# Edge pass of a graph layer with a feed-forward block: three chunks' statistics finished apart, and the second group's reciprocal root moved ahead of a gather

## The chip, the cores and the metric

One core of one Trainium2 chip runs the whole kernel in one launch. The metric is device time in microseconds (us). Before the change the median of three runs is 2741.15 us (2739.52 to 2741.22).

## What is computed

```python
def _layernorm(x, axis=-1, eps=1e-05):
    m = jnp.mean(x, axis=axis, keepdims=True)
    v = jnp.var(x, axis=axis, keepdims=True)
    return (x - m) / jnp.sqrt(v + eps)

# x: (50000, 768); src, dst: 25000 edges, sorted by dst; 12 heads of 64
def gnn(h, src, dst, W, attn_l, attn_r, W_res):
    hv = h.reshape(n, 12, 64)
    ft = jnp.einsum('nhd,od->nho', hv, W)
    a1 = jnp.sum(ft * attn_l, axis=-1)
    a2 = jnp.sum(ft * attn_r, axis=-1)
    e = jax.nn.leaky_relu(a1[src] + a2[dst], negative_slope=0.2)
    m = segment_max(e, dst)
    w = jnp.exp(e - m[dst])
    alpha = w / jnp.maximum(segment_sum(w, dst)[dst], 1e-16)
    agg = segment_sum(alpha[:, :, None] * ft[src], dst)
    return relu((agg + jnp.einsum('nhd,od->nho', hv, W_res)).reshape(n, 768))

x = x + gnn(_layernorm(x), src, dst, ...)
x = x + ffn(_layernorm(x))    # 768 -> 96 -> 768 with gelu; six class rows apart
```

## The kernel before

The kernel has two passes. The **edge pass** takes the 25,000 edges in 196 chunks of 128 (EC = 196), in groups of seven (G = 7) and turns of fourteen (BODY = 14). The **node pass** after it takes 392 tiles of 128 nodes. This change touches the edge pass alone, and there its first two turns.

Every engine has one program, written out by hand, that runs in order; the engines meet at semaphores. Each program loops over the same index `c` (turn `b`, place `i`) and does at `c` the work of chunk `c - LAG` for each of its steps. For one chunk the steps are:

- POOL (GpSimd) issues two gathers by index from `x` in HBM into rings of fourteen slots in `arena`: the 128 source rows (`xs_ring`, line 558, at place c) and the 128 target rows (`xd_ring`, line 536 in `gather_targets`, at place c + 3, DST_LAG). From chunk 14 on it also scatters row numbers into `row_scratch` (line 577), so that a place then has three issues.
- DVE (VectorE) takes mean and variance of the source rows (`source_stats`, lines 982 and 985) when the gather has landed. Once per group, at the place after the group's last chunk, it writes variance + eps of all seven chunks to `ve_s` (line 1061, semaphore `s_ve`).
- POOL raises the seven to the power -0.5 in one instruction into `r_s` (line 586 for the first group, line 592 for the others, at place 18 for the second group; semaphore `s_rp`).
- DVE makes the bias -mean * r in `nm_s` (line 1073, semaphore `s_nm`) and ACT (ScalarE) normalizes the chunk in place (line 668).
- PE (TensorE) transposes source and target rows (line 813), ACT copies the transposes out of PSUM (line 682), PE multiplies (lines 822, 850, 870), ACT copies out again (lines 688, 692) and squares the target rows for their variance (line 700).
- Once per group the attention follows. DVE writes the target variances to `ve_d` (line 1088), POOL raises them to the power -0.5 into `r_d` (line 549, at place 23 for the first group), DVE makes the scores `e_col` from that (lines 1185 to 1193, semaphore `s_leak`), and PE transposes them (line 837, at its place 19) and goes on.
- The sums over edges (lines 864 and 866) start at place 23.

Lines 1185 to 1193 stand in DVE's place 18 behind the statistics of chunk 18, so DVE does nothing else until `r_d` is there. In the same way line 837 stands in PE's program ahead of line 850 of chunk 9, the small product 870 and the transposes of chunk 11.

Ahead of the loop SP starts the loads of the constants and fourteen writes that fill `row_scratch` (3.2 MB, line 453). DVE makes small constants from PE's first products (lines 1020 to 1034). The weights `w1` and `w2` are loaded into the slots of `arena` that `ft_ring` (line 688's output) takes later, and split into high and low parts by DVE right after line 1061 of the first group.

Of the kernel before, what the change touches and what calls it, by code (L numbers as in the profile page):

```python
# [8 lines left out]
D = 768  # L9
# [48 lines left out]
DST_LAG = 3  # L58
HM = HEADS + 1
# [37 lines left out]
def exists(t, n):  # L97

    return not isinstance(t, int) or 0 <= t < n
# [8 lines left out]
def gnn_ffn_kernel(nc, x, x_cols, edges, dst_rows, dst_next, dst_prev, dst_ends, chunk_base, sel_heads,  # L108
# [9 lines left out]
    with ExitStack() as ctx:  # L118
# [60 lines left out]
        w2_sb = part(21504, D, rows=HID + 1)  # L179
        w1_sb = part(24000, NC, HID)  # L180
# [86 lines left out]
        with ExitStack() as edge:  # L267
            agg_ring = edge.enter_context(nc.sbuf_tensor("agg_ring", [P, AR, D], f32))
            dst_all = edge.enter_context(nc.sbuf_tensor("dst_all", [P, G * P], i32))
        row_init = agg_ring[:, AR - 1, 0:NT // BODY * RW].bitcast(i32)  # L270
# [261 lines left out]
        def _(pool):  # L532
# [6 lines left out]
            for b in turns(pool, NB, 2):  # L539
                for i in range(BODY):  # L540
# [21 lines left out]
                    if first and G <= c < G + 4:  # L562
                        for v in (2 * (c - G), 2 * (c - G) + 1):
                            gather_targets(v, v // G, e_all[:, v, 1:2])
                    if exists(cd, EC) and not (isinstance(cd, int) and cd < 8):
                        v = (i - DST_LAG) % BODY
                        e, kd = v // G, v % G
                        n = 2 * b + (i - DST_LAG) // G
                        at_least(pool, s_sqd, cd - BODY + 1)
                        settle(pool)  # L570
                        gather_targets(v, n, e_all[:, v, 1:2] if isinstance(cd, int) and cd < BODY else e_slot[:, e, kd, 1:2])
                        at_least(pool, s_sum, c - BODY - L_SUM + L_TR + 1)
                        settle(pool)
# [10 lines left out]
                    if isinstance(b, int) and c == G + 1:  # L584
                        pool.wait_ge(s_ve, 1)
                        pool.tensor_tensor(r_s[:, 0, :], ve_s[:, 0, :], half[:, 0:G], ALU.pow).then_inc(s_rp, 1)
                    gp = 2 * b + (i - 11) // G
                    if k == 11 % G and exists(gp, NG) and not (isinstance(gp, int) and gp == 0):
                        w = (i - 11) // G % 2
                        pool.wait_ge(s_ve, gp + 1)  # L590
# [63 lines left out]
        def _(act):  # L654
# [5 lines left out]
            for b in turns(act, NB, 2):  # L660
                for i in range(BODY):
                    c = BODY * b + i
                    cn = c - L_NORM
                    if exists(cn, EC):
                        v = (i - L_NORM) % BODY
                        w, k = v // G, v % G
                        act.wait_ge(s_nm, 2 * b + (i - L_NORM) // G + 1)
# [300 lines left out]
        def _(dve):  # L968
# [44 lines left out]

            dve.wait_ge(l_const, 16 * NCONST)
# [7 lines left out]
            for c in range(2):  # L1022
                source_stats(c, c, 0, c, 0)
# [10 lines left out]
            V.tensor_scalar(csr_neg[:], ps[:, 2, 0:P], -1.0, None, ALU.mult).then_inc(s_wgv, 1)  # L1034

# [7 lines left out]
            for b in turns(dve, NB, 2):  # L1043
                for i in range(BODY):
# [13 lines left out]
                    if k == 0 and exists(gv, NG):  # L1058
                        w = (i - 7) // G % 2
                        dve.wait_ge(s_ag, G * (gv + 1))  # L1060
                        V.tensor_scalar(ve_s[:, w, :], mvs[:, w, :, 1], EPS, None, ALU.add).then_inc(s_ve, 1)
# [7 lines left out]
                    if k == 1 and exists(gn, NG):  # L1069
                        w = (i - 8) // G % 2  # L1070
                        dve.wait_ge(s_rp, gn + 1)
                        at_least(dve, s_norm, G * (gn - 1))
                        V.scalar_tensor_tensor(nm_s[:, w, :], mvs[:, w, :, 0], -1.0, r_s[:, w, :],
# [74 lines left out]
                    if exists(c, EC) and not (isinstance(c, int) and c < 2):  # L1148
                        source_stats(c, i, i // G, k, 2 * b + i // G)
# [260 lines left out]
```

## Time and profile before

| | us |
|---|---|
| median of three runs | 2741.15 |
| the profiled execution's own time | 2742.36 |
| its span in the trace | 2740.6 |
| PE busy in the span | 2638.7 (96%) |
| DVE busy | 2397.8 (87%) |
| ACT busy | 2378.1 (87%) |
| POOL busy | 2137.9 (78%) |

Times in the rows count from the span's start. A row of the timeline has start, duration, engine, line, operation, output and inputs, a count, and in brackets how long the engine had been idle before it and what ended that. A DMA row on POOL is the issue of the transfer, not its movement. PEclk is the granted TensorE clock as a share of full speed: 1.00 is 2.4 GHz, 0.50 is 1.2 GHz.

### The profile page before, as it was taken

How to read it: one execution, taken by the hardware profiler on the slowest of the kernel's cores; microseconds unless marked ns; L12 is line 12 of the kernel's file. 1: busy time of each engine (PE TensorE's matmuls, PEld its weight loads, DVE VectorE, ACT ScalarE, POOL GpSimd, SP SyncE). 2: the span in 40 equal slices, each digit the busy share in tenths (PEclk: the TensorE clock that was granted, in tenths of full speed). 3: DMA queues.
4: the chain of work that ended last, by engine and by line, in shares of the span. 5: the costliest groups of instructions: out<-in, count | busy, mean ns of one | idle time of the engine just before them, and what ended most of it. 6: DMA issues, size and time to landing. Idle time of an engine off the chain costs nothing. (4 is left out here: it accounts for less than half of the span.)

```text
span 2740.6 us, 69176 instructions
## 1 busy us (share of the span) xinstructions
PE 2638.7 (96%) x21454; PEld 2393.8 (87%) x21454; DVE 2397.8 (87%) x4888; ACT 2378.1 (87%) x4745; POOL 2137.9 (78%) x2029
## 2 busy tenths in 40 slices
PE   5999999999999974999999999999999999999998
PEld 4888888888888853899999999999999999999996
DVE  4688888888888774999999999999999999999994
ACT  4988888888888844999999999999999999999982
POOL 6777777777777614888888888888888888888881
PEclk9999999999999995999999999999999999999998
DMA  8787777777877637899999999999999999988973
GB/s 312 213 258 253 255 253 255 253 253 253 252 254 253 203 120 254 311 346 345 334 332 331 320 328 327 316 324 318 310 325 318 313 319 313 313 314 312 313 251 126
DMA packets 256712, 777.96 MB, mean 284 GB/s; under 512 B 79719, under 2 KB 87699, under 8 KB 256371
## 3 DMA queue, kind: packets, MB, share of 16 engines
q1 hardware_dynamic: 183980, 563.28, 58.3%
q0 software_dynamic: 69312, 210.37, 24.9%
q8 instruction: 123, 2.02, 0.3%
q10 hardware_dynamic: 3176, 1.29, 0.2%
q14 instruction: 121, 0.99, 0.1%
HBM read 638.90 MB, written 236.69 MB: 319 GB/s over the span
## 5 line engine op out<-in xcount | busy, mean ns | idle before, releaser
L942 PE MATMUL ps<-wr_bd,arena 128*128 128x128 f32 x4704 | 597.8, 277 | 25.2 <-DVE arena L1290 22.6
L942 PEld LDWEIGHTS ps<-wr_bd,arena 128*128 128x128 f32 x4704 | 565.9, 194 | 28.5 <-issue 25.3
L649 POOL DMA_INDIRECT arena<-agg_scratch,nrow x392 | 440.0, 1122 | 79.8 <-issue 67.8
L627 POOL TENSOR_SCALAR arena<-csr_neg,mv,r_n 128x768 f32<-128x768 f32 x392 | 390.1, 995 | 50.9 <-PE ps L796 37.3
L1285 DVE SCALAR_TENSOR_TENSOR ps<-ps,r_n,arena 128x768 f32<-128x768 f32 x392 | 399.0, 1018 | 26.1 <-PE ps L942 17.1
L741 ACT ACTIVATE t_hi<-ps 128x768 fp32r<-128x768 f32 x392 | 315.7, 805 | 85.5 <-PE ps L796 85.4
L1290 DVE SCALAR_TENSOR_TENSOR arena<-ps,arena 128x768 f32<-128x768 f32 x392 | 375.5, 958 | 13.4
L639 POOL TENSOR_SCALAR arena<-arena,nm_n,r_n 128x768 f32<-128x768 f32 x392 | 384.9, 982 | 0.8 <-PE ps L796 0.4
L729 ACT ACTIVATE arena<-arena,mv 128x768 f32<-128x768 f32 x392 | 368.0, 939 | 12.7
L1297 DVE TENSOR_TENSOR t_lo<-ps,t_hi 128x768 fp32r<-128x768 f32 x392 | 373.5, 953 | 2.8 <-ACT t_hi L741 2.7
L750 ACT ACTIVATE arena<-arena,s_st 128x768 f32<-128x768 f32 x392 | 363.4, 927 | 14.2 <-DVE arena L1290 14.2
L1274 DVE TENSOR_TENSOR arena<-arena,ps 128x768 f32<-128x768 f32 x392 | 369.9, 944 | 5.5 <-PE ps L933 5.3
L921 PE MATMUL ps<-t_hi,w_hi 128*96 128x256 f32 x1176 | 360.0, 306 | 0.0
L921 PE MATMUL ps<-t_lo,w_hi 128*96 128x256 f32 x1176 | 329.7, 280 | 0.0
L921 PE MATMUL ps<-t_hi,w_lo 128*96 128x256 f32 x1176 | 328.4, 279 | 0.0
L767 ACT ACTIVATE arena<-arena 128x768 f32<-128x768 f32 x392 | 326.0, 832 | 0.6
L796 PE MATMUL ps<-ident,arena 128*128 128x128 f32 x2352 | 321.8, 273 | 1.9 <-POOL arena L639 1.1
L813 PE MATMUL ps<-ident,arena 128*128 128x128 f32 x2352 | 298.5, 277 | 13.2 <-ACT arena L668 13.2
L682 ACT ACTIVATE arena<-ps 128x512 f32<-128x512 f32 x588 | 304.4, 588 | 2.4 <-PE ps L813 2.3
L822 PE MATMUL ps<-wgv,arena 128*128 128x130 f32 x2352 | 296.7, 275 | 0.0
L577 POOL DMA_INDIRECT row_scratch<-e_slot x182 | 206.8, 1136 | 110.7 <-issue 39.8
L813 PEld LDWEIGHTS ps<-ident,arena 128*128 128x128 f32 x2352 | 272.8, 149 | 13.5 <-issue 13.5
(208 smaller groups left out, 6160.9 us busy)
## 6 DMA issues: line engine op xcount, KB each, us to landing
arena<-in_x SPq DMA_DIRECT2D x196, 768.0 KB
arena<-in_x_cols SPq DMA_DIRECT2D x392, 384.0 KB, 5.1
out<-arena SPq DMA_DIRECT2D x195, 768.0 KB, 5.8
agg_scratch<-agg_ring SPq DMA_DIRECT2D x196, 384.0 KB, 3.0
dst_all<-in_dst_rows SPq DMA_DIRECT2D x28, 256.0 KB, 4.0
arena<-agg_scratch,nrow POOLq DMA_INDIRECT x392
arena<-in_x,e_slot POOLq DMA_INDIRECT x364, 4.6
dst_all<-in_dst_rows SPq DMA_DIRECT2D x28, 192.0 KB
```

What stands on the lines that cost most here:

```text
L627: pool.tensor_scalar(g_ring[:, g, :].rearrange("p (c f) -> p c f", f=P), csr_neg[:, None, :].to_broadcast([P, NC, P]), mv1[:, w, 2 * (v % ...
L639: pool.tensor_scalar(n2[:, v % 2, :], y_ring[:, v, :], nm_n[:, w, k:k + 1], r_n[:, w, PAIR + k:PAIR + k + 1], ALU.add, ALU.mult).then_inc( ...
L649: pool.indirect_dma_start(g_ring[:, g, :], None, agg_d, bass.IndirectOffsetOnAxis(nrow[:, v, 3:4], 0), bounds_check=EP - 1, oob_is_err=Fal ...
L729: nc.scalar.activation(junk[:, 0, :], x_ring[:, v, :], ACT.Square, bias=mv1[:, w, 2 * k:2 * k + 1], scale=-1.0, accum_out=q_st[:, w, k:k + ...
L750: nc.scalar.activation(junk[:, 1, :], y_ring[:, v, :], ACT.Square, bias=s_st[:, w, k:k + 1], scale=-float(D), accum_out=q_st[:, w, 2 + k:3 ...
L813: last = nc.tensor.transpose(ps[:, k, m % 4 * P:(m % 4 + 1) * P], src[:, v, m % NC * P:(m % NC + 1) * P], ident[:])
L921: last = nc.tensor.matmul(ps[0:HID, 6 + v, 0:PAIR * P], w[:, i, :], h[:, i, :], start=(i == 0 and n == 0), stop=(i == NC - 1 and n == 2))
L942: last = nc.tensor.matmul(pair(1)[:, i * P:(i + 1) * P], xt_ring[:, g, i * P:(i + 1) * P], wr_bd[:], start=True, stop=True)
L1274: V.tensor_tensor(y_ring[:, v, :], y_ring[:, v, :], pair(2), ALU.add).then_inc(s_o, 1)
L1285: V.scalar_tensor_tensor(pair(1), pair(1), r_n[:, w, k:k + 1], g_ring[:, g, :], ALU.mult, ALU.add).then_inc(s_z1, 1)
L1290: V.scalar_tensor_tensor(y_ring[:, v, :], pair(1), 0.0, x_ring[:, v, :], ALU.max, ALU.add, accum_out=s_st[:, w5, k:k + 1]).then_inc(s_y, 1)
L1297: V.tensor_tensor(t2_lo[:, v, :, f], pair(0).rearrange("p (c n) -> p c n", c=NC), t2_hi[:, v, :, f].bitcast(f32), ALU.subtract).then_inc(s ...
```

## The change

The first group's power is taken in two parts: chunks 0 to 2 (E0 = 3) apart, and chunks 3 to 6. On DVE the statistics of chunks 0 and 1 go ahead of the constants, those of chunk 2 and their variance + eps behind the four copies of line 1020, and the bias of the three chunks behind the other constants. On POOL the first power stands at place 4, behind the gather of source chunk 4, and the second at the end of place 7. The target gathers of chunks 0 to 7, which went in pairs at places 7 to 10, now go one at a time at places 3 to 10. The second group's power goes from the end of place 18 to the end of place 13, ahead of the gathers of chunk 14. `w1` and `w2` are loaded into two slots of `agg_ring` in place of `ft_ring`'s.

```diff
+E0 = 3
...
-        w2_sb = part(21504, D, rows=HID + 1)
-        w1_sb = part(24000, NC, HID)
...
+        w2_sb = agg_ring[0:HID + 1, 0, :]
+        w1_sb = agg_ring[:, 1, 0:NC * HID].rearrange("p (c h) -> p c h", h=HID)
...
                     cd = c - DST_LAG
-                    if first and G <= c < G + 4:
-                        for v in (2 * (c - G), 2 * (c - G) + 1):
-                            gather_targets(v, v // G, e_all[:, v, 1:2])
-                    if exists(cd, EC) and not (isinstance(cd, int) and cd < 8):
+                    if first and c == E0 + 1:
+                        pool.wait_ge(s_ve, 1)
+                        pool.tensor_tensor(r_s[:, 0, 0:E0], ve_s[:, 0, 0:E0], half[:, 0:E0], ALU.pow).then_inc(s_rp, 1)
+                    if exists(cd, EC):
...
-                        at_least(pool, s_sum, c - BODY - L_SUM + L_TR + 1)
-                        settle(pool)
+                        if not isinstance(cd, int) or cd >= 8:
+                            at_least(pool, s_sum, c - BODY - L_SUM + L_TR + 1)
+                            settle(pool)
...
-                    if isinstance(b, int) and c == G + 1:
-                        pool.wait_ge(s_ve, 1)
-                        pool.tensor_tensor(r_s[:, 0, :], ve_s[:, 0, :], half[:, 0:G], ALU.pow).then_inc(s_rp, 1)
+                    if isinstance(b, int) and c == G:
+                        pool.wait_ge(s_ve, 2)
+                        pool.tensor_tensor(r_s[:, 0, E0:G], ve_s[:, 0, E0:G], half[:, E0:G], ALU.pow).then_inc(s_rp, 1)
+                    if isinstance(b, int) and c == BODY - 1:
+                        pool.wait_ge(s_ve, 3)
+                        pool.tensor_tensor(r_s[:, 1, :], ve_s[:, 1, :], half[:, 0:G], ALU.pow).then_inc(s_rp, 1)
...
-                    if k == 11 % G and exists(gp, NG) and not (isinstance(gp, int) and gp == 0):
+                    if k == 11 % G and exists(gp, NG) and not (isinstance(gp, int) and gp < 2):
...
+            for c in range(2):
+                source_stats(c, c, 0, c, 0)
             dve.wait_ge(l_const, 16 * NCONST)
             dve.wait_ge(s_pre, 1)
...
-            for c in range(2):
-                source_stats(c, c, 0, c, 0)
+            source_stats(2, 2, 0, 2, 0)
+            dve.wait_ge(s_ag, E0)
+            V.tensor_scalar(ve_s[:, 0, 0:E0], mvs[:, 0, 0:E0, 1], EPS, None, ALU.add).then_inc(s_ve, 1)
             dve.wait_ge(s_pre, 2)
...
+            dve.wait_ge(s_rp, 1)
+            V.scalar_tensor_tensor(nm_s[:, 0, 0:E0], mvs[:, 0, 0:E0, 0], -1.0, r_s[:, 0, 0:E0],
+                                   ALU.mult, ALU.mult).then_inc(s_nm, 1)
```

The waits on `s_ve`, `s_rp` and `s_nm` count one more from then on, and ACT's first three normalizations wait for the first count of `s_nm`.

POOL around the second group's power, before. Line 558 is a source gather, 536 a target gather, 577 a scatter; the first row is the gather of source chunk 17, and the power is line 592.

```order
L558 DMA arena<-in_x,e_slot 128x768
L536 DMA arena<-in_x,e_slot 128x768
L577 DMA row_scratch<-e_slot 50176x16
L558 DMA arena<-in_x,e_slot 128x768
L536 DMA arena<-in_x,e_slot 128x768
L577 DMA row_scratch<-e_slot 50176x16
L592 TENSOR_TENSOR r_s<-ve_s,half 128x7
```

POOL around the same power, with the change (559 is the source gather, 537 the target gather, 579 the scatter, 591 the power). The first row is the gather of source chunk 13.

```order
L559 DMA arena<-in_x,e_all 128x768
L537 DMA arena<-in_x,e_all 128x768
L591 TENSOR_TENSOR r_s<-ve_s,half 128x7
L559 DMA arena<-in_x,e_slot 128x768
L537 DMA arena<-in_x,e_all 128x768
L559 DMA arena<-in_x,e_slot 128x768
L537 DMA arena<-in_x,e_all 128x768
L559 DMA arena<-in_x,e_slot 128x768
L537 DMA arena<-in_x,e_all 128x768
L559 DMA arena<-in_x,e_slot 128x768
L537 DMA arena<-in_x,e_slot 128x768
L579 DMA row_scratch<-e_slot 50176x16
```

The power is twelve issues further forward: six of chunks 14 to 16 and two times three of chunks 17 and 18 now stand behind it. Between this power and `r_d`'s there are now 24 issues, and no power.

POOL at the start of the loop, with the change, from the gather of target chunk 0 on (565 and 588 are the two parts of the first group's power):

```order
L537 DMA arena<-in_x,e_all 128x768
L559 DMA arena<-in_x,e_all 128x768
L565 ISA
L565 TENSOR_TENSOR r_s<-ve_s,half 128x3
L537 DMA arena<-in_x,e_all 128x768
L559 DMA arena<-in_x,e_all 128x768
L537 DMA arena<-in_x,e_all 128x768
L559 DMA arena<-in_x,e_all 128x768
L537 DMA arena<-in_x,e_all 128x768
L559 DMA arena<-in_x,e_all 128x768
L537 DMA arena<-in_x,e_all 128x768
L588 TENSOR_TENSOR r_s<-ve_s,half 128x4
```

Six gathers stand ahead of the first power, where thirteen stood before, and seven between the two parts.

## Rows read from the trace of the kernel before

**Rows 1.** Page, busy time; then busy us by stretch: PE, PEld, DVE, ACT, POOL, PEclk.
```profile
PE 2638.7 (96%) x21454; PEld 2393.8 (87%) x21454; DVE 2397.8 (87%) x4888; ACT 2378.1 (87%) x4745; POOL 2137.9 (78%) x2029
...
50.00:100.00 50.00, 39.69 (x382) 35.55 (x381) 20.04 (x69) 42.83 (x82) 38.95 (x37) 0.93 0.62 184
100.00:150.00 50.00, 50.00 (x434) 41.35 (x433) 41.65 (x103) 43.94 (x82) 38.07 (x34) 1.00 0.82 252
```
**Rows 2.** Timeline of PE, chunk 5's last product to the score transposes of line 837.
```profile
61.50 0.57 PE L870 MATMUL ps<-arena 96*128 96x13 f32 x2 [4.71 <-ACT arena L692]
61.92 2.80 PE L813 MATMUL ps<-ident,arena 128*128 128x128 f32 x12
...
68.52 1.51 PE L813 MATMUL ps<-ident,arena 128*128 128x128 f32 x12
...
72.80 1.50 PE L813 MATMUL ps<-ident,arena 128*128 128x128 f32 x12
...
78.36 1.51 PE L822 MATMUL ps<-wgv,arena 128*128 128x130 f32 x12
79.71 0.27 PE L837 MATMUL ps<-ident,e_col 128*84 128x128 f32 x1
```
**Rows 3.** Busy time by stretch, the PEclk behind that idle time (third number from the end).
```profile
60.00:65.00 5.00, 3.50 (x17) 3.53 (x18) 1.48 (x6) 4.57 (x10) 3.78 (x5) 0.50 0.69 211
```
**Rows 4.** Timeline of DVE, second group's bias, and first scores from r_d.
```profile
57.81 0.17 DVE L1073 SCALAR_TENSOR_TENSOR nm_s<-mvs,r_s 128x7 f32<-128x7 f32 x1 [7.07 <-POOL r_s L592]
...
76.02 0.17 DVE L1185 TENSOR_TENSOR nmd<-a_all,r_d 128x7 f32<-128x7 f32 x1 [1.21 <-POOL r_d L549]
...
76.66 0.25 DVE L1193 SCALAR_TENSOR_TENSOR e_col<-e_col 128x84 f32<-128x84 f32 x1
```
**Rows 5.** Timeline of POOL: source gather 14, second group's power, gather 22, r_d, third group's power.
```profile
41.31 0.94 POOL L558 DMA_INDIRECT arena<-in_x,e_slot  x1 [0.30 <-PE ps L813]
...
56.21 1.56 POOL L592 TENSOR_TENSOR r_s<-ve_s,half 128x7 f32<-128x7 f32 x1
...
70.88 0.98 POOL L558 DMA_INDIRECT arena<-in_x,e_slot  x1 [1.57 <-PE ps L813]
...
74.44 1.55 POOL L549 TENSOR_TENSOR r_d<-ve_d,half 128x7 f32<-128x7 f32 x1
...
87.55 1.53 POOL L592 TENSOR_TENSOR r_s<-ve_s,half 128x7 f32<-128x7 f32 x1
```
**Rows 6.** Timeline of POOL at the start: source gather 5, the first power, gather behind it.
```profile
12.64 0.95 POOL L558 DMA_INDIRECT arena<-in_x,e_all  x1 [0.30 <-issue]
...
23.69 1.75 POOL L586 TENSOR_TENSOR r_s<-ve_s,half 128x7 f32<-128x7 f32 x1 [1.34 <-DVE ve_s L1061]
25.65 1.48 POOL L558 DMA_INDIRECT arena<-in_x,e_all  x1 [0.20 <-issue]
```
**Rows 7.** Timeline of DVE, statistics of chunks 1, 2, 6 and 9.
```profile
13.35 0.99 DVE L982 BATCH_NORM_STATS2 bn_a<-arena 128x6 f32<-128x384 f32 x2
...
16.27 1.01 DVE L982 BATCH_NORM_STATS2 bn_a<-arena 128x6 f32<-128x384 f32 x2
...
22.12 0.97 DVE L982 BATCH_NORM_STATS2 bn_a<-arena 128x6 f32<-128x384 f32 x2
...
32.55 1.02 DVE L982 BATCH_NORM_STATS2 bn_a<-arena 128x6 f32<-128x384 f32 x2 [3.68 <-DMA arena<-in_x,e_all]
```
**Rows 8.** Gathers from x, issue to landing: from 0 to 60 us; from 55 to 100 us.
```profile
DMA to landing us min/median/max: 3.8/6.7/8.4
...
DMA to landing us min/median/max: 3.8/4.3/4.7
```
**Rows 9.** Timeline of DVE and ACT: statistics of chunk 13; normalization of chunks 7 and 14.
```profile
45.36 1.01 DVE L982 BATCH_NORM_STATS2 bn_a<-arena 128x6 f32<-128x384 f32 x2
...
58.01 1.03 ACT L668 ACTIVATE arena<-arena,nm_s,r_s 128x768 f32<-128x768 f32 x1 [4.09 <-DVE nm_s L1073]
...
91.43 1.03 ACT L668 ACTIVATE arena<-arena,nm_s,r_s 128x768 f32<-128x768 f32 x1 [0.54 <-DVE nm_s L1073]
```

More of the change, by code:

```diff
@@ L583, in _ @@
                             .then_inc(d_scat_first, 16)
-                    if isinstance(b, int) and c == G + 1:
-                        pool.wait_ge(s_ve, 1)
-                        pool.tensor_tensor(r_s[:, 0, :], ve_s[:, 0, :], half[:, 0:G], ALU.pow).then_inc(s_rp, 1)
+                    if isinstance(b, int) and c == G:
[4 more added lines that the diff above has]
+                        pool.tensor_tensor(r_s[:, 1, :], ve_s[:, 1, :], half[:, 0:G], ALU.pow).then_inc(s_rp, 1)
                     gp = 2 * b + (i - 11) // G
-                    if k == 11 % G and exists(gp, NG) and not (isinstance(gp, int) and gp == 0):
+                    if k == 11 % G and exists(gp, NG) and not (isinstance(gp, int) and gp < 2):
                         w = (i - 11) // G % 2
-                        pool.wait_ge(s_ve, gp + 1)
+                        pool.wait_ge(s_ve, gp + 2)
                         settle(pool)
@@ L666, in _ @@
                         w, k = v // G, v % G
-                        act.wait_ge(s_nm, 2 * b + (i - L_NORM) // G + 1)
+                        act.wait_ge(s_nm, 1 if isinstance(cn, int) and cn < E0 else 2 * b + (i - L_NORM) // G + 2)
                         nc.scalar.activation(xs_ring[:, v, :], xs_ring[:, v, :], ACT.Identity,
@@ L1060, in _ @@
                         dve.wait_ge(s_ag, G * (gv + 1))
-                        V.tensor_scalar(ve_s[:, w, :], mvs[:, w, :, 1], EPS, None, ALU.add).then_inc(s_ve, 1)
+                        lo = E0 if isinstance(gv, int) and gv == 0 else 0
+                        V.tensor_scalar(ve_s[:, w, lo:], mvs[:, w, lo:, 1], EPS, None, ALU.add).then_inc(s_ve, 1)
                         if isinstance(gv, int) and gv == 0:
@@ L1070, in _ @@
                         w = (i - 8) // G % 2
-                        dve.wait_ge(s_rp, gn + 1)
+                        lo = E0 if isinstance(gn, int) and gn == 0 else 0
+                        dve.wait_ge(s_rp, gn + 2)
                         at_least(dve, s_norm, G * (gn - 1))
-                        V.scalar_tensor_tensor(nm_s[:, w, :], mvs[:, w, :, 0], -1.0, r_s[:, w, :],
+                        V.scalar_tensor_tensor(nm_s[:, w, lo:], mvs[:, w, lo:, 0], -1.0, r_s[:, w, lo:],
                                                ALU.mult, ALU.mult).then_inc(s_nm, 1)
@@ L1146, in _ @@
                         V.tensor_scalar(gap, gap, 0.0, -100.0, ALU.min, ALU.max).then_inc(s_gap, 1)
-                    if exists(c, EC) and not (isinstance(c, int) and c < 2):
+                    if exists(c, EC) and not (isinstance(c, int) and c < E0):
                         source_stats(c, i, i // G, k, 2 * b + i // G)
```

## The prediction

> **What bounds the kernel now.** The busy shares come first, then the same by stretch [rows 1]. Over the span PE is busy 96%. From 100 us on it is busy all 50.00 us of a stretch, so a shift that PE has by then stays to the end of the edge pass, and the node pass starts that much sooner or later. Between 50 and 100 us PE works 39.69 of 50: this is the fill, and only here can the change gain or lose. So the question is when PE comes to a point that everything later follows from. I take its line 837, the first group's score transposes, at 79.71 us [rows 2], and two waits ahead of it.
>
> The first is PE's stand of 4.71 us before 61.50 [rows 2]. DVE waited 7.07 us for the second group's power, which POOL ran from 56.21 to 57.77 [rows 4, 5], and chunk 7 was normalized at 58.01 [rows 9]. During the stand the granted clock fell to 0.50, which is 1.2 GHz [rows 3]. So chunk 7 took 6.60 us from its transposes to those of chunk 8 (61.92 to 68.52), where the next took 4.28 [rows 2]: 2.3 us for the clock.
>
> The second is short, but everything turns on it. DVE waited 1.21 us for `r_d`, the target power, which POOL ran from 74.44 to 75.99 [rows 4, 5]. The scores were done at 76.66 + 0.25 = 76.91, 0.92 us after that power, and PE came to line 837 at 79.71 without a wait [rows 2, 4]. So POOL had 2.8 us to spare there, no more. `r_d` stands behind all gathers up to chunk 22 in POOL's program.
>
> **The change, step by step.** I follow POOL, since the three powers now each wait in its program for data that it has itself sent for a little earlier. One gather costs POOL 0.95 + 0.30 = 1.25 us [rows 6].
>
> *First power.* Its gathers are six, the last issued at 12.64 to 13.59 [rows 6]. The three chunks' statistics end with chunk 2. Chunk 1's start when it has landed, at 13.35 at the latest; with 1.25 for them and 0.5 for the four copies, DVE is free for chunk 2 at 15.1. That chunk had landed by 16.27 [rows 7]. I take 15.7, the middle. From the start of a chunk's statistics to the power were 1.57 us (22.12 to 23.69) and the power 1.75 [rows 6, 7]: it runs from 17.3 to 19.0. POOL stands from 13.6 to 17.3.
>
> *Second part.* After a power the first gather is issued 0.21 later, and took 1.48 where others take 0.95 [rows 6]. So target 1 goes at 19.2, source 5 at 21.0, source 6 at 23.5, and target 4, the last before the wait, ends at 28.2. The power needs source 6. Gathers took 3.8 to 8.4 us to land in the first 60 us and 4.3 in the middle later on [rows 8]. The nearest row is chunk 9's gather, the first after POOL's old pause: issued at 25.65, waited for until 32.55, 6.9 us [rows 6, 7]. The new pause is longer, so less is queued ahead: I take 6.0. It lands at 29.5, the power starts at 31.1 and ends at 32.65 (1.55 us, as in rows 5).
>
> *Second group.* Source 13 is the eleventh issue after that, at 32.85 + 10 x 1.25 = 45.35; target 10 ends at 47.55. By then the loads of the start are mostly over, so I take the later middle value, 4.3 us [rows 8]: chunk 13 lands at 49.65 (it had landed by 45.36 before [rows 9]), the power starts 1.6 later, 51.3, and ends at 52.85. This is 4.9 us sooner than the 57.77 of before, as the change has it. But POOL stood from 47.55 to 51.3, and what is queued behind the wait is source 14 and everything after it: it goes at 53.05, where it went at 41.31 [rows 5], **11.7 us later**.
>
> *Chunk 7.* DVE makes its bias at place 15, behind the statistics of chunk 14. That gather lands at 53.05 + 4.3 = 57.35; with 1.25 and 0.2 for the bias, chunk 7 is normalized at 58.9. Before it was 58.01 [rows 9]. So the early power gives chunk 7 nothing, and PE's stand ahead of it with its clock remains. That chunks 0 to 6 run earlier ends in a longer wait here.
>
> *`r_d`.* From source 14 to `r_d` were 74.44 - 41.31 = 33.1 us. In them were the power (1.56) and 1.27 us beyond the usual 0.30 of waiting for PE at chunk 22 [rows 5]; both are gone, 30.3 remain for the 24 issues. So `r_d` runs from 83.35 to 84.9, the scores end at 85.8, and PE's line 837 goes at 85.9 instead of 79.71: **6.2 us later**. DVE does nothing else meanwhile, and in PE's program the products and transposes of chunks 9 and 11 stand behind line 837.
>
> *The clock.* PE's work ahead of line 837 ended at 79.87 before [rows 2]; with chunk 7 0.9 later it ends at 80.8. PE then stands 5.1 us. That is more than the 4.71 after which the clock fell [rows 2, 3], and the two grow together, since both hang on source 14. I count the fall at chunk 7's **2.3 us**.
>
> *Later.* The third group's power started 13.1 us after `r_d`'s (87.55 - 74.44) and takes 1.53 [rows 5]: it now ends at 98.0, so chunk 14 is normalized at 98.2 at the earliest, 6.8 later than its 91.43 [rows 9]. With 6.2 + 2.3 = 8.5 on PE this floor is hidden. POOL needs about 3 x 1.25 us a chunk, less than PE, so it catches up afterwards.
>
> *At nothing.* Three more small instructions on DVE lie in waits for gathers [rows 7]. One power more on POOL is in the times above. The weights' new place has no other user until chunk 0's sums.
>
> Sum: the median 2741.15 + 8.5 = **2749.7 us**, 0.3% slower. The profiled execution took 2742.36, 1.2 above the median; the change is counted on the median.
>
> *A rule weighed.* The rows show a gather of 393 KB landing after 3.8 us at the shortest [rows 8]. The Trainium skill, "DMA: Bandwidth & Descriptors", section "Anatomy of one DMA — SWDGE (gpsimd) path", gives 2.0 us and the bytes at 436 GB/s, an estimate of 2.9 us here, and then the three waits shrink until the sum is 4.5 us instead of 8.5, 2745.7. No run here shows 2.9. By the rows, 6.0 and 4.3 stand.
>
> **Rivals.**
>
> *Gathers land fast.* If POOL's pauses empty the DMA queues, source 6 and 13 land in 3.8 us [rows 8], and chunk 2 by 15.1. Then the first power ends at 18.4, source 6 goes at 22.9 and lands at 26.7, the second power runs 28.3 to 29.85, source 13 goes at 42.55, lands at 46.35, the third power ends at 49.5, source 14 goes at 49.7. Line 837 comes at 82.6, 2.9 late, 5.2 with the clock: 2746.3; without the clock the chunk 14 floor gives 3.4, 2744.6. For it speaks that the pause leaves the queue to the loads; against it, that the same bytes had chunk 13 landing at 45 with POOL never waiting long.
>
> *The clock stays up.* Then the floor at chunk 14 holds: 6.8 us, 2748.0. Against it speaks the 4.71 us stand.
>
> *The early start carries through.* If source 14 goes early enough, chunk 7's bias is what counts. With source 14 at 49.7, chunk 7 is normalized at 55.0, 3.0 us sooner, and PE's stand of 4.7 shrinks to 1.7, so the 2.3 of the clock may go too: 5.3 us faster, 2735.8. That only stays if line 837 can go at 74.4, so `r_d` must start by 71.9, 30.3 us after source 14, which would have to go by 41.6. Beyond that point POOL's queue decides, and three waits for gathers stand ahead of it.
>
> *It does nothing.* If PE's pace in the fill hides the shift: 2741.2. Line 837 without a wait now [rows 2] and only 2.8 us to spare speak against it.
>
> **How the numbers follow.** About 0.2% (5.5 us) is what a measurement here can tell from no change. Forecast 0.55, fast gathers 0.20, clock up 0.15, early start 0.06, nothing 0.04. Forecast and clock up are slower by over 0.2%: 0.70. Fast gathers and nothing are within it: 0.24. The early start stands for faster: 0.06. The range takes in fast gathers without the clock's price, 2744.6, rounded down to 2744. At the upper end, chunk 2 at 16.27 adds 0.6, source 6 at 8.4 us 2.4, source 13 at 6.7 us 2.4. I take in about 4.5 of these 5.4: 2754. Nothing, the early start and a little above are left out.
>
> **What would show it.** In the new profile: POOL's three powers near 17, 31 and 51 us, each after a wait for DVE; source gather 14 near 53; chunk 0's transposes some 8 us sooner than before; chunk 7's normalization near 59; DVE waiting some 9 us for `r_d`, with its power near 83; PE standing about 5 us before line 837 near 86 and at 0.50 behind it. Wrong it is if source 14 goes before 47 us, or if PE reaches line 837 without waiting.

## The result, and the profile after

The changed kernel takes 2754.64 us (median of five runs, 2752.22 to 2758.98), the kernel before 2741.22 beside it. The ratio is 1.0051, with a 95% interval of 1.0036 to 1.0066. So the change costs 13.4 us where 8.5 were predicted; the direction held, and the time lies 0.6 us above the range.

In the code of the change lines have moved: 842 is the old 837, 818 the old 813, 875 the old 870, 1073 the old 1061, 1086 the old 1073, 1108 the old 1095, 1198 to 1206 the old 1185 to 1193.

The page, and busy time by stretch as in [rows 1]:

```profile
PE 2644.9 (96%) x21454; PEld 2397.8 (87%) x21454; DVE 2399.7 (87%) x4890; ACT 2378.9 (86%) x4745; POOL 2139.2 (78%) x2030
...
50.00:100.00 50.00, 37.83 (x342) 33.81 (x342) 15.85 (x59) 37.18 (x71) 34.74 (x35) 0.86 0.63 193
100.00:150.00 50.00, 48.37 (x434) 40.79 (x433) 38.00 (x97) 45.28 (x86) 38.73 (x34) 1.00 0.74 227
```

The work is the same; the fill holds less of it. Between 50 and 100 us PE does 1.9 us less than before, at 0.86 of full clock instead of 0.93, and it still has gaps behind 100 us.

Timeline of POOL, from the first power to `r_d` (answers to [rows 5, 6]):

```profile
18.22 0.89 POOL L565 TENSOR_TENSOR r_s<-ve_s,half 128x3 f32<-128x3 f32 x1 [4.53 <-DVE ve_s L1031]
...
23.17 0.96 POOL L559 DMA_INDIRECT arena<-in_x,e_all  x1 [0.30 <-issue]
...
32.83 1.28 POOL L588 TENSOR_TENSOR r_s<-ve_s,half 128x4 f32<-128x4 f32 x1 [4.91 <-DVE ve_s L1073]
...
47.22 0.95 POOL L559 DMA_INDIRECT arena<-in_x,e_all  x1 [0.30 <-issue]
...
55.42 1.51 POOL L591 TENSOR_TENSOR r_s<-ve_s,half 128x7 f32<-128x7 f32 x1 [6.00 <-DVE ve_s L1073]
57.13 1.02 POOL L559 DMA_INDIRECT arena<-in_x,e_slot  x1 [0.20 <-issue]
...
87.63 1.55 POOL L550 TENSOR_TENSOR r_d<-ve_d,half 128x7 f32<-128x7 f32 x1
```

The three waits are there: 4.53, 4.91 and 6.00 us. The gathers shown are those of source 6, source 13 and source 14. Source 14, behind the third wait, goes at 57.13 instead of 41.31, and `r_d` follows at 87.63 instead of 74.44.

Timeline of PE, from the small product of chunk 1 to the transposes of chunk 12 (answers to [rows 2]):

```profile
46.85 0.61 PE L875 MATMUL ps<-arena 96*128 96x13 f32 x2 [11.32 <-DVE a_all L1108]
...
67.56 0.57 PE L875 MATMUL ps<-arena 96*128 96x13 f32 x2 [2.32 <-ACT arena L697]
...
83.39 1.51 PE L827 MATMUL ps<-wgv,arena 128*128 128x130 f32 x12
90.15 0.44 PE L842 MATMUL ps<-ident,e_col 128*84 128x128 f32 x1 [5.25 <-DVE e_col L1206]
92.28 0.57 PE L875 MATMUL ps<-arena 96*128 96x13 f32 x2 [0.47 <-ACT arena L697]
92.70 2.80 PE L818 MATMUL ps<-ident,arena 128*128 128x128 f32 x12
95.29 2.81 PE L827 MATMUL ps<-wgv,arena 128*128 128x130 f32 x12
99.26 0.36 PE L875 MATMUL ps<-arena 96*128 96x13 f32 x2 [0.56 <-ACT arena L697]
99.48 1.51 PE L818 MATMUL ps<-ident,arena 128*128 128x128 f32 x12
```

PE stands 5.25 us before line 842 and reaches it 10.44 us later than before. Behind the stand the clock is at 0.50, the lower of the two levels (1.2 GHz), in busy time by stretch:

```profile
90.00:95.00 5.00, 4.38 (x27) 3.55 (x28) 3.94 (x15) 2.78 (x6) 3.78 (x5) 0.50 0.52 158
```

so chunk 11's transposes take 2.80 us instead of 1.51. In the kernel before, the last small product of these rows (chunk 10's, ahead of the transposes of chunk 12) stood here:

```profile
85.87 0.36 PE L870 MATMUL ps<-arena 96*128 96x13 f32 x2 [1.11 <-ACT arena L692]
```

From the scores to that product PE needs 9.11 us (90.15 to 99.26) instead of 6.16 (79.71 to 85.87). This adds 2.95 us, and from chunk 12 on PE is 13.4 us late. The shift stays: the last score transposes of the edge pass, before and now, start 13.38 us apart.

```profile
1003.19 0.31 PE L837 MATMUL ps<-ident,e_col 128*84 128x128 f32 x1
```
```profile
1016.57 0.31 PE L842 MATMUL ps<-ident,e_col 128*84 128x128 f32 x1
```

This comparison, row by row within the edge pass, leaves out the node pass and is used below as **the shift**. It rests on one profiled execution of each kernel, and the start of a kernel scatters too. In the six runs whose programs are the same up to there (the change, e1, e3, e4, e7 and e11) the first power started between 16.92 and 18.22 us and its second part between 31.15 and 32.83. So two shifts that differ by less than some 1.7 us are not told apart.

New, and not predicted, are the 11.32 us before 46.85. Timeline of DVE, statistics of chunk 6, of chunk 10, of chunk 13, first scores (answers to [rows 4, 7, 9]):

```profile
31.21 1.02 DVE L987 BATCH_NORM_STATS2 bn_a<-arena 128x6 f32<-128x384 f32 x2 [1.28 <-DMA arena<-in_x,e_all]
...
45.43 1.02 DVE L987 BATCH_NORM_STATS2 bn_a<-arena 128x6 f32<-128x384 f32 x2
...
46.68 0.12 DVE L1108 COPY a_all<-ps 128x13 f32<-128x13 f32 x1
...
53.20 0.17 DVE L1108 COPY a_all<-ps 128x13 f32<-128x13 f32 x1 [2.74 <-PE ps L875]
...
53.81 1.01 DVE L987 BATCH_NORM_STATS2 bn_a<-arena 128x6 f32<-128x384 f32 x2
...
89.21 0.17 DVE L1198 TENSOR_TENSOR nmd<-a_all,r_d 128x7 f32<-128x7 f32 x1 [9.32 <-POOL r_d L550]
```

The two copies take the small products of chunks 0 and 2 out of PSUM. In DVE's program the first stands behind the statistics of chunk 10, and the second ahead of those of chunk 13. PE has the product of chunk 0 early now, but can't go on before DVE has copied it; DVE then stands 2.74 us for the product of chunk 2, and only then takes chunk 13's statistics, on which POOL's third wait hangs. The gather was not what they waited for. Source gather 13 alone, from its issue at 47.22 to its landing:

```profile
DMA to landing us min/median/max: 4.3/4.3/4.3
```

It was there at 51.5, 2.3 us before the statistics began.

Timeline of ACT, normalization of chunks 7 and 14 (answers to [rows 9]):

```profile
64.07 1.03 ACT L673 ACTIVATE arena<-arena,nm_s,r_s 128x768 f32<-128x768 f32 x1 [1.70 <-DVE nm_s L1086]
...
104.82 1.03 ACT L673 ACTIVATE arena<-arena,nm_s,r_s 128x768 f32<-128x768 f32 x1 [0.53 <-DVE nm_s L1086]
```

Both are later than before (58.01 and 91.43): the early power gains chunk 7 nothing.

### The profile page after: what moved, and what is told of

It is laid out like the page before. It is cut to its first block and busy times, and to the rows that moved or that the text cites. A ratio compares the mean times of both kernels' runs of the same rounds, so it can differ in the third digit from the quotient of the medians.

```text
span 2755.5 us, 69227 instructions
## 1 busy us (share of the span) xinstructions
PE 2644.9 (96%) x21454; PEld 2397.8 (87%) x21454; DVE 2399.7 (87%) x4890; ACT 2378.9 (86%) x4745; POOL 2139.2 (78%) x2030
## 5 line engine op out<-in xcount | busy, mean ns | idle before, releaser
L1303 DVE SCALAR_TENSOR_TENSOR arena<-ps,arena 128x768 f32<-128x768 f32 x392 | 375.3, 957 | 13.4
L734 ACT ACTIVATE arena<-arena,mv 128x768 f32<-128x768 f32 x392 | 368.0, 939 | 12.7
L755 ACT ACTIVATE arena<-arena,s_st 128x768 f32<-128x768 f32 x392 | 363.4, 927 | 14.3 <-DVE arena L1303 14.3
L827 PEld LDWEIGHTS ps<-wgv,arena 128*128 128x128 f32 x2352 | 281.1, 192 | 0.0
```

What stands on the lines that cost most here:

```text
L734: nc.scalar.activation(junk[:, 0, :], x_ring[:, v, :], ACT.Square, bias=mv1[:, w, 2 * k:2 * k + 1], scale=-1.0, accum_out=q_st[:, w, k:k + ...
L827: last = nc.tensor.matmul(ft_ps[:, n // 3, n % 3, :], both_t[:, v, n * P:(n + 1) * P], wgv[:, n, :], start=True, stop=True)
L1303: V.scalar_tensor_tensor(y_ring[:, v, :], pair(1), 0.0, x_ring[:, v, :], ALU.max, ALU.add, accum_out=s_st[:, w5, k:k + 1]).then_inc(s_y, 1)
```

## The experiments

Each run was timed beside the kernel before on the same chip; an interval that holds 1.0000 (e5 and e6) tells no difference. The shift is given at the first and at the last score transposes.

| run | median us | ratio (95%) | shift, first / last |
|---|---|---|---|
| the change | 2754.64 | 1.0036 to 1.0066 | +10.4 / +13.4 |
| e1_pow1_back | 2749.72 | 1.0022 to 1.0041 | +7.3 / +7.3 |
| e2_pow1_alone | 2746.9 | 1.0012 to 1.0046 | +1.8 / +3.8 |
| e3_rd_early | 2753.66 | 1.0030 to 1.0064 | +5.1 / +14.3 |
| e4_rd_pow2_early | 2752.45 | 1.0028 to 1.0056 | +4.2 / +9.4 |
| e7_copies_early | 2749.17 | 1.0023 to 1.0047 | +7.3 / +9.5 |
| e8_rowfill_late | 2759.47 | 1.0049 to 1.0080 | +14.8 / +17.3 |
| e10_rowfill_half | 2754.93 | 1.0029 to 1.0057 | +10.7 / +12.7 |
| e13_rowfill_half_copies | 2752.3 | 1.0029 to 1.0059 | +6.8 / +9.0 |
| e5_pow1_place16 | 2739.52 | 0.9987 to 1.0005 | -4.5 / -2.1 |
| e6_pow1_16_rd_21_pow2_23 | 2738.35 | 0.9983 to 1.0001 | -7.4 / -4.2 |
| e9_rd_place28 | 2735.84 | 0.9976 to 0.9994 | -7.1 / -4.0 |
| e11_split_rest_early | 2744.12 | 1.0007 to 1.0026 | +0.1 / +3.2 |
| e12_rd_place29 | 2735.02 | 0.9968 to 0.9986 | -5.8 / -4.5 |

### Each half alone

The second group's power goes back to place 18, the split stays:

```diff
-                    if isinstance(b, int) and c == BODY - 1:
-                        pool.wait_ge(s_ve, 3)
-                        pool.tensor_tensor(r_s[:, 1, :], ve_s[:, 1, :], half[:, 0:G], ALU.pow).then_inc(s_rp, 1)
...
```

> The change without its last part: the second group's power stands at the end of place 18 again, the first group's two parts stay. Theory (POOL's waits for statistics push back everything queued behind them, and PE is held at line 842 by the late r_d): source gather 14 goes near 49.7 us instead of 57.1, r_d's power starts near 80, PE does not wait at line 842. What is late instead is the second group's power itself, near 65 to 66.5, so chunk 7 is normalized near 66.7 (58.0 before), 8.6 us late, and the clock falls there as in the kernel before: 8.6 us over before, 2749.8. Rival (the loss is the early start alone: PE's stand of 11.3 us behind DVE's copy for chunk 0, and the early second power is a gain): taking the gain away makes it slower than the change, 2756 or more.

Measured 7.6 us slower by the medians (2742.13 beside it), shift +7.3. It went as the theory said: source 14 at 48.45 instead of 41.31, the second group's power at 63.43 instead of 56.21, and PE came to its scores at 87.04 without a wait. Then the other half, before with the power at the end of place 13:

```diff
+                    if isinstance(b, int) and c == BODY - 1:
+                        pool.wait_ge(s_ve, 2)
+                        pool.tensor_tensor(r_s[:, 1, :], ve_s[:, 1, :], half[:, 0:G], ALU.pow).then_inc(s_rp, 1)
...
```

> The kernel before with only the second group's power moved, to the end of place 13. Theory: POOL waits there until chunk 13's statistics are done, near 47, the power ends near 48.5, source gather 14 goes at 48.7 instead of 41.3; chunk 7 is normalized near 54.5, 3.5 us sooner than 58.0, and PE's stand before it is gone; but r_d starts near 79 instead of 74.4, so PE stands some 7 us before its line 837, goes there near 81.6 instead of 79.7, and the clock falls there at about 3 us: 4.9 us over before, 2746.1. Rival (the early second power is a gain, the loss lies in the first group's part): 3.5 to 5.8 us under before, 2735.4 to 2737.7.

Timeline of POOL and of DVE in this run:

```profile
46.98 1.52 POOL L589 TENSOR_TENSOR r_s<-ve_s,half 128x7 f32<-128x7 f32 x1 [6.57 <-DVE ve_s L1064]
...
79.02 1.55 POOL L549 TENSOR_TENSOR r_d<-ve_d,half 128x7 f32<-128x7 f32 x1
```
```profile
80.60 0.17 DVE L1188 TENSOR_TENSOR nmd<-a_all,r_d 128x7 f32<-128x7 f32 x1 [11.78 <-POOL r_d L549]
```

The power comes 9.2 us sooner than in [rows 5], POOL stands 6.57 us for it, and `r_d` comes 4.6 later. Both halves lose by themselves: 7.3 and 3.8, together 11.1 of the 13.4.

### r_d ahead of the queue

In the change, the first `r_d` goes from place 23 to the start of place 21; then, in a second run, the third group's power also goes from place 25 to the end of place 23.

```diff
+                    if isinstance(b, int) and c == 21:
+                        pool.wait_ge(s_ved, 1)
...
+                    if isinstance(b, int) and c == 23:
+                        pool.wait_ge(s_ve, 4)
...
```

> The change with one instruction moved: the first group's r_d power goes from POOL's place 23 to the start of its place 21. Theory: it runs near 80 to 81.5 instead of 87.6 to 89.2, the scores are done near 82.4, and PE reaches line 842 near 84.8 without a wait. The next thing late is then the third group's power, which still ends near 102.3 behind the same gathers: chunk 14 is normalized near 102.5, 11.1 us later than before. So PE stands at chunk 14 instead, and the time is 11 us over before, 2752.3, or up to 2755 if the clock falls there. Rival (line 842 is not what holds PE, the early start is): line 842's wait goes or stays, the time is that of the change, 2754.6, and the wait does not turn up at chunk 14.

> As the run before, and the third group's power goes from POOL's place 25 to the end of place 23. Theory: it now ends near 95, so chunk 14 is normalized near 96.4 with no wait, and PE runs from line 842 on without a stand and at full clock: 5.0 us over before, 2746.2. Rival (the early start is what is lost): the time is that of the change, 2754.6.

The first came out as expected: `r_d` ran at 79.98, the 5.25 us at the scores were gone, and in their place PE stood 7.27 us before the small product at 106.16 (chunk 12's), as the third group's power came only at 100.90.

```profile
79.98 1.54 POOL L554 TENSOR_TENSOR r_d<-ve_d,half 128x7 f32<-128x7 f32 x1
```
```profile
106.16 0.57 PE L879 MATMUL ps<-arena 96*128 96x13 f32 x2 [7.27 <-ACT arena L701]
```

The second was a miss: +9.4, where +5.0 was expected. Its shift was +4.2 until PE came to the second group's scores; there POOL was late again. Timelines of POOL and PE in it:

```profile
117.53 1.52 POOL L550 TENSOR_TENSOR r_d<-ve_d,half 128x7 f32<-128x7 f32 x1
```
```profile
120.03 0.31 PE L850 MATMUL ps<-ident,e_col 128*84 128x128 f32 x1 [3.14 <-DVE e_col L1214]
```

So a late POOL meets one consumer after the other. Once the sums over edges have begun, POOL takes some 3.84 us from chunk to chunk for its issues and PE 4.89 (source gathers 97.32 and 101.16, transposes 97.60 and 102.49 in e6 below), so POOL makes up 1 us a chunk.

### What held the second group's power back

The prediction had source 14 at 53.05; it went at 57.13. Two suspects: the landing of the gathers, and DVE's copies. First the copies of chunks 0 to 2, moved forward to places 8, 10 and 11:

```diff
+                    if isinstance(b, int) and c in (8, 10, 11):
+                        j = {8: 0, 10: 1, 11: 2}[c]
+                        dve.wait_ge(s_sct, j + 1)
+                        V.tensor_copy(a2_all[:, 0, j, :], a2_ps).then_inc(s_a2c, 1)
...
```

> The change with DVE's copies of chunk 0's, 1's and 2's small product moved from places 11, 12 and 13 to places 8, 10 and 11. Theory: PE's stand of 11.3 us before chunk 1's small product shrinks to some 4.6, and chunk 13's statistics no longer wait for PE (53.8) but start when its gather lands, near 51.5; the second group's power ends near 54.6 instead of 56.9 and everything behind it, r_d and line 842, comes 2.3 us sooner: 11.1 us over before instead of 13.4. Rival (PE's long stand is itself the loss): PE's 6.7 us go over to the end, 6.7 over before.

Shift +9.5; the stand before chunk 1's product fell from 11.32 to 6.55, and source 14 went at 53.94, 3.2 us sooner than in the change. Chunk 13's statistics now wait for their gather, and for PE no longer:

```profile
50.61 1.02 DVE L987 BATCH_NORM_STATS2 bn_a<-arena 128x6 f32<-128x384 f32 x2 [1.02 <-DMA arena<-in_x,e_all]
```

The gather was issued at 46.10, so they start 4.5 us behind it instead of 6.6. These 2.1 us are what the copies had cost, near the 2.3 of the theory. The other 1.1 of the 3.2 were there already when source 13 was issued: the first power came at 17.45 here instead of 18.22, ahead of anything that the edit touches, and its second part at 31.70. That is scatter of the start. The fall from +13.4 to +9.5 has 0.7 more from the clock, which cost 2.2 us in this run. Then the writes into `row_scratch`, held back:

```diff
             sp.wait_ge(s_rowinit, 1)
+            sp.wait_ge(s_ag, BODY)
...
-                        if isinstance(b, int) and c == BODY:
+                        if isinstance(b, int) and c == BODY + DST_LAG:
                             pool.wait_ge(d_rowinit, 16 * BODY)
```

> The change with SP's fourteen writes that fill row_scratch held back until chunk 13's statistics are done, and POOL's wait for them at place 17 instead of 14. Theory (source gather 6 took 8 us to land because those writes share the DMA engines): it lands some 4.3 us after its issue, the second part of the first group's power ends near 30 instead of 34.1, all gathers behind it go some 4 us sooner, and line 842 too: some 9.3 us over before instead of 13.4. Rival (a gather takes that long by itself then): 13.4 over before.

The first half came true: source 6, issued at 21.64, had its statistics at 26.04, 4.4 us behind the issue instead of 8.0, and source 14 went at 52.57.

```profile
21.64 0.96 POOL L560 DMA_INDIRECT arena<-in_x,e_all  x1 [0.30 <-issue]
```
```profile
26.04 1.02 DVE L988 BATCH_NORM_STATS2 bn_a<-arena 128x6 f32<-128x384 f32 x2 [1.23 <-DMA arena<-in_x,e_all]
```

But the writes then ended late, and POOL stood for them before the first scatter:

```profile
71.61 1.03 POOL L580 DMA_INDIRECT row_scratch<-e_slot  x1 [9.19 <-DMA row_scratch<-agg_ring]
```

So the sum was a miss: the price had moved, not gone. Next, the writes were held for seven chunks only (`G` in place of `BODY` in the added wait), without the copies, and then with them:

> The change, with the fourteen writes that fill row_scratch held back on SP until seven source chunks have had their statistics, and POOL's wait for them moved from place 14 to place 17 (in e8 they were held for fourteen chunks, and POOL then stood 9.2 us before the first scatter). Theory (those writes are what makes source 6 land after 8 us, and this costs the second part of the first power 4 to 5 us, which r_d hands on): source 6 lands in about 4.3 us, the second part of the power is at 27.7, source 14 is issued near 52.6 and POOL does not stand before the first scatter; r_d near 83, PE's line 842 near 85.6, +5.9 against before, with the clock's 3.0 about +9 us, 2750. Rival 1 (the writes cost the same wherever they lie): source 13 now lands after some 8 us, source 14 at 56 to 57, +12 to +13.5, 2753 to 2754.5. Rival 2 (they have nothing to do with the landing; the first time was chance): source 6 lands in 8 us again, +13.4.

> The change, with two things together: the row_scratch writes held until seven source chunks have had their statistics (as in e10_rowfill_half) and DVE's copies of the small products of chunks 0 to 2 at places 8, 10 and 11 (as in e7_copies_early). In e10 source 13 was issued at 43.20, 4.0 us sooner than in the change, but its statistics still came at 54.07, after DVE had stood 4.00 us for PE's small product of chunk 2. Theory (the two together are what the prediction lacked: the landing of source 6, and DVE's program, which held chunk 13's statistics behind those copies): chunk 13's statistics near 49, the second group's power near 50.5, source 14 issued near 52.3, r_d near 83, PE's line 842 near 85.5, 5.8 us late, with the clock's 3 about +8.8, 2750. Rival 1 (DVE's copies are not it; source 13 itself lands late): source 14 at 56 to 57 again, +12.7, 2754. Rival 2 (PE, now not standing in the 40s, keeps its lead): under +5.

Timeline of DVE in e10_rowfill_half, the copy of chunk 2 and the statistics of chunk 13:

```profile
53.46 0.17 DVE L1109 COPY a_all<-ps 128x13 f32<-128x13 f32 x1 [4.00 <-PE ps L876]
...
54.07 1.01 DVE L988 BATCH_NORM_STATS2 bn_a<-arena 128x6 f32<-128x384 f32 x2
```

and of DVE and POOL in e13_rowfill_half_copies:

```profile
50.21 1.02 DVE L988 BATCH_NORM_STATS2 bn_a<-arena 128x6 f32<-128x384 f32 x2 [0.96 <-DMA arena<-in_x,e_all]
```
```profile
51.84 1.51 POOL L592 TENSOR_TENSOR r_s<-ve_s,half 128x7 f32<-128x7 f32 x1 [6.97 <-DVE ve_s L1074]
53.54 1.02 POOL L560 DMA_INDIRECT arena<-in_x,e_slot  x1 [0.20 <-issue]
```

In the first, source 13 was issued at 43.20, 4.0 us sooner than in the change, and its statistics came no sooner. It landed after 7.4 us, at 50.6, and DVE stood 4.00 us for PE and took them at 54.07. In the second, nothing but the copies differs, and they come 3.9 sooner, on the gather's landing (issued at 42.56, so 7.6 us: the writes had moved beside it). Source 14 is at 53.54, PE's scores (the change's line 842) at 86.51, the shift +9.0. This is near the prediction's own numbers (53.05, 85.9, +8.5), but in part by luck: source 13 was issued 2.8 us sooner than predicted and took 3.3 longer to land. The copies alone gave +9.5 (e7), so what moving the writes adds is not told apart from nothing. By the whole time the run is 10.7 us slower, its interval 8 to 16.

### The powers early where nothing is waited for

The power may go early without a wait: before, with it at the end of place 16, where the data are there.

```diff
+                    if isinstance(b, int) and c == 16:
+                        pool.wait_ge(s_ve, 2)
+                        settle(pool)
+                        pool.tensor_tensor(r_s[:, 1, :], ve_s[:, 1, :], half[:, 0:G], ALU.pow).then_inc(s_rp, 1)
...
```

> The kernel before with only the second group's power moved, from place 18 to the end of place 16, where its data is there (near 48.6 us), so that POOL does not wait. Theory (the loss of the change is POOL's waiting, not the early power): chunk 7 is normalized near 54.0 instead of 58.0 and PE's stand and its half clock are gone; r_d starts near 73 and not later than before, so PE may stand up to 3 us at line 837, at some 75.8 instead of 79.7; 3.4 us under the kernel before. Rival (an early second power brings the loss, wherever it stands): slower than before.

The power ran at 48.14 without a wait, chunk 7 was normalized at 54.30, and PE came to the scores 4.5 us sooner. Then 2.4 of it went. Timeline of PE, its stands before the scores and before chunk 12's small product:

```profile
75.22 0.31 PE L841 MATMUL ps<-ident,e_col 128*84 128x128 f32 x1 [1.61 <-DVE e_col L1197]
...
91.16 0.36 PE L874 MATMUL ps<-arena 96*128 96x13 f32 x2 [1.86 <-ACT arena L696]
```

Up to the second of them 0.7 was lost, where the kernel before had stood 1.17 us at the same place (94.92), and behind it 1.7, as the clock fell. By the whole time the run is not told apart from the kernel before. Busy time by stretch, of this run and of the kernel before:

```profile
90.00:95.00 5.00, 3.84 (x23) 3.87 (x24) 2.82 (x10) 4.30 (x9) 3.88 (x4) 0.73 0.69 219
```
```profile
90.00:95.00 5.00, 3.71 (x39) 3.38 (x40) 3.71 (x11) 4.46 (x9) 3.99 (x4) 1.00 0.58 157
```

Next, with the first `r_d` at place 21 and the third group's power at place 23 as well:

> As the run before it, with the first r_d power at the start of place 21 and the third group's power at the end of place 23. Theory: PE reaches line 837 near 73.0 without a stand; the next consumer of POOL's program is the second group's r_d, which still ends near 107 where PE would come to line 837 near 105.8, so some 2.4 us are given back there: 4.3 us under the kernel before. If POOL's order has nothing to do with it: the same as the run before it.

> The kernel before with the second group's power at the end of place 16, the third group's at the end of place 23, the first group's r_d at the start of place 21 and the second group's at the start of place 28; all other powers as before. It differs from e6_pow1_16_rd_21_pow2_23 in the last of these alone, which stood at place 29 there. In that run POOL raised the second group's r_d at 104.70, though ve_d had been written at 97.53, DVE stood 5.10 us for it and PE 1.89 before the second score transposes, which came 5.25 us ahead of the kernel before instead of 7.38, and the lead of PE ended at 4.23 us. Theory (POOL's place in the queue alone is late there, not its data): r_d at about 100.9, no stand of PE before the second score transposes, PE's lead stays at 7 us or a little less, and the time is 6 to 7 us below the kernel before, about 2734.5 (ratio 0.9977). Rival (POOL as a whole is behind, and the next consumer stands in turn, as in e4): the lead falls to about 4 us again at the third group, 2737.

In the first of these the lead was 7.4 us at the first scores, 5.3 at the second, as the second group's `r_d` still ran at 104.70, and 4.2 at the third. The second of these runs was meant to move that `r_d` too (from place 30, not 29), but its turn runs as a loop, where an edit for one place has no effect. So e6 and e9 are the same program twice, with leads of 4.2 and 4.0 and ratios of 0.9992 and 0.9985. The second tells nothing of its theory, but it does tell how far two runs of one program agree. In e12 `r_d` of every group but the first goes one place earlier in the loop itself:

```diff
-                    gd = 2 * b + (i - L_VD - 5) // G
+                    gd = 2 * b + (i - L_VD - 4) // G
...
```

> e9_rd_place28 did not move the second group's r_d: the place it named lies in the turns that run as a loop, where an edit for one place has no effect, and so its program is that of e6. Here r_d of every group but the first goes one place earlier in the loop (29, 36 and so on), and the first stays at place 21. Theory: the second group's r_d runs at about 101 instead of 104.9, PE has no stand of 1.9 us before the second score transposes, its lead stays near 7 us instead of 4.0, and the time is some 6 to 7 us below the kernel before, about 2735. Rival (POOL is behind as a whole and the next consumer stands in turn): the lead still falls to 4 us, 2737.

By its median this is the fastest version, and it beats both kernels: 6.6 us below the kernel before by the medians, ratio 0.9977. The edge pass accounts for 4.5 of it; what lies beyond is within what whole runs of one program differ by. Timelines of POOL and PE in it:

```profile
48.81 1.54 POOL L595 TENSOR_TENSOR r_s<-ve_s,half 128x7 f32<-128x7 f32 x1
...
102.41 1.52 POOL L549 TENSOR_TENSOR r_d<-ve_d,half 128x7 f32<-128x7 f32 x1
```
```profile
73.88 0.27 PE L850 MATMUL ps<-ident,e_col 128*84 128x128 f32 x1
...
106.71 0.27 PE L850 MATMUL ps<-ident,e_col 128*84 128x128 f32 x1
```

PE no longer stands before the second scores, and the lead there is the same as at the first, 5.8. It began 1.3 us smaller than in e9 and lost 1.1 at the third group, so against e9 the gain in shift is only 0.5, and by the whole time the two are not told apart. The theory held for the stand, not for the 7 us.

Last, the split on top of early powers (the edit for the second `r_d` has no effect here either, so its places are those of e6 and e9):

> The change's first half alone (three chunks' statistics and power apart, targets one at a time), with the powers behind it where e9_rd_place28 has them: the second group's at the end of place 16, the first r_d at the start of place 21, the third group's power at the end of place 23, the second r_d at the start of place 28. It tells what the split itself is worth when nothing behind it is late in POOL's queue. Theory (the split only makes POOL stand some 8 us for two powers in the first 35 us, and starts chunks earlier that then wait at chunk 7): chunk 7 is normalized near 57 to 58, PE's first score transposes come 0 to 2 us ahead of the kernel before, the time is 2739 to 2741.5, some 5 us above e9. Rival (chunks 0 to 6 done 8 us sooner do carry through once r_d is not late): PE's lead is 7 us or more, 2734 or less.

Measured 2744.12, 2.6 us above what was expected; the rival fell. The shift is +3.2, so 7.3 us worse than e9 with the same places. The split costs 7.3 by itself (e1) and 7.3 here, but not by the same path. In e11 no late power holds PE. Timelines of PE, the small products of chunks 1 and 2 in e11, and that of chunk 2 in e9:

```profile
45.18 0.60 PE L885 MATMUL ps<-arena 96*128 96x13 f32 x2 [11.59 <-DVE a_all L1118]
...
51.22 0.36 PE L885 MATMUL ps<-arena 96*128 96x13 f32 x2 [0.60 <-ACT arena L707]
```
```profile
43.98 0.36 PE L883 MATMUL ps<-arena 96*128 96x13 f32 x2 [0.59 <-ACT arena L705]
```

PE stood 11.59 us for DVE's copy of chunk 0's small product, as in the change, and the clock behind the stand was granted at 0.61 (45 to 50 us). At chunk 2's product PE was 7.24 us behind e9, and at the first scores still 7.25, with no wait longer than 0.60 between. The copies stood at their old places here. The split with prompt powers and with the copies moved as in e7 was not run, so what it is worth then is open.

## Why the prediction came out as it did

- *Bound and chain:* right. POOL stands three times, source 14 and all behind it slip, `r_d` is late, PE stands at line 842. From source 14 to `r_d` were 30.5 us (30.3 predicted), from `r_d` to line 842 2.52 (2.55).
- *First power:* it started at 18.22, 0.9 behind the 17.3 predicted. Chunk 2's statistics waited for their gather until 16.60, later than the latest time considered (16.27). But the power on three columns took 0.89 us and not 1.75, so it ended at 19.11, where 19.0 was predicted. The two misses cancel, which is luck.
- *Second part:* 32.83, not 31.1. Source 6 went at 23.17, 0.3 sooner than predicted, but took 8.0 us to land, not the 6.0 chosen; the longest of the rows, 8.4 [rows 8], was nearer. This term was mis-sized. With the writes held back it took 4.4 (e8).
- *Second group:* this is the step that failed. Of the 4.1 us by which source 14 was later than predicted, 1.9 had come down from the second part (source 13 at 47.22, not 45.35). The other 2.2 are in the wait itself: I let chunk 13's statistics start when the gather had landed, 4.3 us after its issue. It did land after 4.3 us, at 51.5. They started at 53.81, since DVE's program holds them behind the copy of chunk 2's small product, and that waited for a PE which DVE itself had held up for 11.32 us. I had read POOL's program for what stands behind a wait, but not DVE's for what stands ahead of these statistics. e7 shows it: with the copies moved they start on the landing, and the shift falls to 9.5. e10 and e13 agree: with source 13 sooner but the copies in place the statistics came no sooner, and with the copies moved too the shift came to 9.0.
- *Chunk 7:* no gain, as said; 64.07 instead of 58.9, as source 14 was 4.1 later and took 5.5 us to its statistics (57.13 to 62.67), not 4.3.
- *The clock:* it fell as said, after a stand of 5.25 us, and cost 2.95 instead of 2.3.
- *Later:* chunk 14 did not bind, and POOL's backlog stayed hidden behind PE's own delay. e3 and e4 show that it is there once the scores are not late.
- *Sum:* 10.44 + 2.95 = 13.4 in place of 6.2 + 2.3 = 8.5. Of the 4.9 us between them, 1.9 come from the second part, 2.2 from chunk 13's statistics, 0.65 from the clock, and the rest from source 14 to `r_d`.
- *Rivals:* fast gathers fell (8.0 us), and so did the clock staying up. The early start did not carry through in any run with the split. Prompt powers alone do not bring it about: in e11 PE is at the scores 7.3 us behind the same kernel without the split. But there it is DVE's copy of chunk 0 that holds PE, so it is not shown that the early start must fail with the copies moved too.
- *The rule weighed:* source gathers of the change, issue to landing in the first 60 us (answers to [rows 8]):

```profile
DMA to landing us min/median/max: 4.0/5.3/8.1
```

  The time counts from the start of POOL's issue. No gather came near 2.9 us. The estimate from the Trainium skill, "DMA: Bandwidth & Descriptors", section "Anatomy of one DMA — SWDGE (gpsimd) path", does not hold here, and the measurement decides. The sum that I gave for it is off as well: with 2.9 in place of 6.0 and of 4.3, source 14 goes 4.5 us sooner, and 8.5 less 4.5 is 4.0, not 4.5.

Not shown is what a landing costs when nothing else moves; the writes were shifted, not left out.

## What to carry to other kernels

Before an instruction moves forward on an in-order queue, ask whether its data are there at the new place: placed three chunks later, where no wait came, the same power gained 4.5 us at the scores; placed where POOL waited 6.6 us for them, it lost 1.8 there. Follow the chain backwards through every engine's program, the one that makes the data too, since a wait can hold up the engine on which it waits itself. A backlog on such a queue shows up at its next consumer when the first is mended, so look at two or three consumers before counting a gain.

## What was not expected

- The same gather landed after 8.0 us beside the `row_scratch` writes and 4.4 us without them (source 6, the change and e8). When the writes were moved, the long landing moved along: 7.6 us for source 13 in e13.
- PE's clock fell in e5 after stands of 1.61 and 1.86 us and took 1.7 us of a 4.5 us lead. In e6 a stand of 1.89 us before the second scores, behind two of 1.18 and 1.16, did not bring it down (granted 1.00 from 105 to 115 us). Why it fell in one and not in the other stays open.
- A shift that PE has at the third group's scores stays to 0.02 us over the next 25 groups, except in e12, which gave back 0.14 on the way.
